# GIN stage of a four-layer graph network: ranks of edges by two passes over the bins, normalisations that read PSUM, y's bias rows in banks of their own

## The chip, the cores and the metric

One core of a Trainium2 chip runs the whole program in one launch. The metric is the device time in microseconds (us) of an execution, median of several. The engines are TensorE (PE; its weight loads are PEld), VectorE (DVE), ScalarE (ACT), GpSimd (POOL) and SyncE (SP), each with a queue of its own that is worked off in order; a wait holds everything behind it in the same queue.

## What is computed

Four graph networks in a row, each with a residual sum and a layer norm behind it, on 3125 nodes of 128 features and 53125 edges (sorted by target). The change touches the first one, GIN, of four layers:

```python
def _bn(x, g, b):
    m = jnp.mean(x, axis=0)
    v = jnp.var(x, axis=0)
    return g * (x - m) * jax.lax.rsqrt(v + BN_EPS) + b
src, dst = (edge_index[0], edge_index[1])
for l in range(L):                                      # L = 4, hidden width 32
    S = jax.ops.segment_sum(X[src], dst, num_segments=N_NODES)
    Z = (1.0 + eps[l]) * X + S
    h = jax.nn.relu(_bn(Z @ W1[l].T + b1[l], g1[l], bt1[l]))
    h = jax.nn.relu(_bn(h @ W2[l].T + b2[l], g2[l], bt2[l]))
    X = h @ W3[l].T + b3[l]
...
x = _layernorm(x + _L0_gnn_ref(x, ...), axis=-1)
x = _layernorm(x + _L1_gnn_ref(x, edge_attr_64, ...), axis=-1)
x = _layernorm(x + _L2_gnn_ref(x, ...), axis=-1)
x = _layernorm(x + _L3_gnn_ref(x, edge_attr_20, ...), axis=-1)
```

The fourth network needs the edges in another order, by source. The kernel sorts them itself, and does so inside the GIN stage.

## The kernel before

The program is a row of stages with a barrier of all engines between them: `prepare`, `adjacency`, `gin`, `layernorm`, and then the other networks. A stage ends when the last of its queues is through.

`prepare` and `adjacency` make the dense matrix of edge counts `adj` (3125 by 3125, f16, 25 tiles of 125 source nodes) in SBUF. `prepare` also leaves, in `extra`, the tables of the ranks: `bins` (125 partitions by 425 columns, f32: the bin, source // 125, of each edge), and two triangular bf16 matrices `before` and `upto`.

`gin` does two things at once.

**The layers.** The 3125 nodes stand as four groups of 32 features over up to 875 columns, so that a layer's hidden values h fill 128 partitions. A layer l makes y (per slot of 125 nodes, 32 wide; L884 for l = 0, L892 after), in PSUM banks 0 and 1; splits it in parts (`parts`, L748 to L750, or `parts16`, L745); multiplies the 25 slots with `adj`, in 7 pieces of up to 450 columns in banks 0 to 6 (L908, L917; L924); copies the sums to SBUF (pieces 0, 2, 4 by ScalarE, L817; pieces 1, 3, 5, 6 by VectorE, L774); and merges them to z in banks 7 and 0 (L943, L951). Then come two normalisations: ScalarE adds the bias and moves z from PSUM to `zb` in SBUF (L823), VectorE takes statistics of `zb` (L713 to L716), TensorE spreads mean and variance over the groups (L875, L877), VectorE makes scale and shift, ScalarE applies them with a relu (L829). Between the two stands the product by W2 (L959). Bias rows for the next y are put in banks 0 and 1 (L968) when the second normalisation has left PSUM. After the last layer L974 makes X, and L787, L833 add its bias.

**The ranks.** For each of 25 bins u in turn: VectorE marks the edges of the bin (`hots`, L664), TensorE counts with `before` and `upto` (two products of 426 columns, L848 and L849), ScalarE copies the counts (L796), VectorE scans along the 426 columns, carrying on from the bin before (L672), and chooses the marked ones (L679); GpSimd adds them to `places_f` (L641). Four bins run ahead of the layers, the other 21 are interleaved with the first layer's product, one per slot, TensorE putting the counts between the slots. Between the fourth and the fifth, VectorE makes the joined weights (L732 to L738). The 7 copies of sums of the first layer wait for the last bin (`s_placed` at L767 and L810). Then VectorE turns the places into row numbers (L777 to L781).

SP's queue in this stage: the loads, x first; a wait for all 7 copies (L614, L615); the row of degrees to HBM (L616); the places to HBM (L618); and then it fills, in 14 turns of 8 chunks, rows of edge data and places. GpSimd's queue, behind the 25 adds: 14 x 8 = 112 indirect DMAs (L647) that write 125 edge rows each to `edge_rows`. The remaining 313 are done in a later stage (L1637). The wait for places that opens this is:

```python
eng.wait_ge(s_sa, len(ACT_P))
eng.wait_ge(s_sv, len(DVE_P))
eng.dma_start(G["deg_row"][:, :], S[3 * GH:3 * GH + 1, :]).then_inc(s_deg, 16)
eng.wait_ge(s_places, 1)
eng.dma_start(places[:, :], place_i).then_inc(s_saved, 16)
eng.wait_ge(s_saved, 16)
```

## Time and profile before

| | us |
|---|---|
| median of 3 runs (2288.94 to 2290.55) | 2289.44 |
| the profiled execution | 2289.18 |
| its span in the trace | 2287.5 |
| mean granted TensorE clock, share of full | 0.782 |
| `prepare` and `adjacency` | 0 to 242.99 |
| `gin` | 242.99 to 528.03 |
| busy over the span: PE, DVE, ACT, POOL | 81%, 60%, 51%, 59% |

Times in rows are from the start of the span. A row of the timeline has start, duration, engine (SPq is a DMA issue by SyncE), line, operation, what it writes and reads, how often it stands there, and in brackets how long its engine had been idle and what ended that. The TensorE clock has two levels, 1.2 and 2.4 GHz; PEclk is the mean of what was granted, 1.00 being the higher.

### The profile page before, as it was taken

The page shows a single profiled execution, that of the slowest core. Times are in us where ns is not written, and L with a number is a line of the kernel's source. Part 1 is how long each engine was busy: PE and PEld are TensorE (multiplying, and loading weights), DVE is VectorE, ACT ScalarE, POOL GpSimd, SP SyncE. Part 2 cuts the span into 40 slices and gives each one's busy share as a digit, 9 for nine tenths or more (in the row PEclk, how much of TensorE's full clock was granted, in tenths as well). Part 3 has the DMA queues.
Part 4 walks back from the last instruction along what each step waited for, and adds up shares of the span by engine and source line. Part 5 has one row for each costly group of instructions (what it writes and reads, how often), then busy time and mean ns, then how long its engine had stood idle before and what let it go on. Part 6 is the DMA issues. An engine that isn't in the chain of part 4 may idle for free. (4 is left out here: it accounts for less than half of the span.)

```text
span 2287.5 us, 41999 instructions
## 1 busy us (share of the span) xinstructions
PE 1858.7 (81%) x8353; PEld 1333.2 (58%) x8353; DVE 1371.2 (60%) x4157; ACT 1169.0 (51%) x2626; POOL 1353.6 (59%) x1334
## 2 busy tenths in 40 slices
PE   3888677776799899999889989989986666767767
PEld 2666444445788888888555545545564454555544
DVE  6999592223444444444366576577557777777775
ACT  2999112222566666676353083073035666666663
POOL 1000136771677777777147877777726777777771
PEclk9999697887655555555679999999987777677787
DMA  0000101112344444444211111111142222222221
GB/s 12 0 0 0 45 1 18 18 17 65 96 120 118 119 119 120 119 121 121 62 40 18 19 16 18 20 17 17 20 147 67 64 64 65 64 65 65 64 65 41
DMA packets 193722, 128.61 MB, mean 56 GB/s; under 512 B 138397, under 2 KB 174886, under 8 KB 192753
## 3 DMA queue, kind: packets, MB, share of 16 engines
q0 software_dynamic: 40256, 60.21, 12.1%
q1 hardware_dynamic: 150631, 59.16, 10.1%
q10 hardware_dynamic: 2636, 7.10, 0.9%
q8 instruction: 62, 1.02, 0.2%
q14 instruction: 137, 1.12, 0.2%
HBM read 106.83 MB, written 13.34 MB: 53 GB/s over the span
## 5 line engine op out<-in xcount | busy, mean ns | idle before, releaser
L2210 POOL DMA_INDIRECT adj<-h_rows,adj x416 | 395.7, 951 | 154.9 <-issue 74.0
L1250 POOL DMA_INDIRECT extra<-p_rows,small x416 | 393.8, 947 | 136.6 <-issue 106.8
L1637 POOL DMA_INDIRECT edge_rows<-pay,small x313 | 381.7, 1219 | 98.7 <-issue 94.6
L1445 PE MATMUL ps<-work 128*128 x1024 | 302.5, 450 | 50.5 <-ACT work L1381 47.4
L2427 PE MATMUL ps<-adj 128*128 128x125 f32 x928 | 208.8, 363 | 157.9 <-DVE adj L2305 155.7
L2427 PEld LDWEIGHTS ps<-adj 128*128 128x128 f32 x928 | 172.1, 255 | 255.4 <-issue 161.2
L1445 PEld LDWEIGHTS ps<-work 128*128 128x128 f32 x1024 | 235.0, 318 | 75.4 <-issue 73.3
L1324 DVE TENSOR_TENSOR work<-ps,extra 128x256 f32<-128x256 f32 x256 | 108.7, 425 | 239.0 <-PE ps L1445 213.1
L1456 PEld LDWEIGHTS ps<-small,work 128*128 128x128 f32 x1024 | 243.6, 326 | 1.7 <-issue 0.7
L1456 PE MATMUL ps<-small,work 128*128 128x64 f32 x1024 | 240.8, 390 | 0.6 <-issue 0.5
L1999 PE MATMUL ps<-adj,work 125*128 (+2 forms) x1008 | 205.9, 361 | 21.2 <-DVE work L1728 21.2
L1999 PE MATMUL ps<-adj,extra 125*128 (+2 forms) x1092 | 214.9, 352 | 0.0
L487 PE MATMUL ps<-work 125*125 125x500 bf16 x628 | 162.8, 402 | 39.6 <-DVE work L418 39.1
L2417 PE MATMUL ps<-adj 112*128 112x256 f32 x464 | 190.1, 502 | 1.0 <-ACT adj L2350 1.0
L2295 DVE SCALAR_TENSOR_TENSOR adj<-adj 128x128 f32<-128x128 f32 x464 | 143.9, 350 | 67.3 <-POOLq L2215 55.6
L1378 ACT ACTIVATE work<-work 64x256 f32<-64x256 int32 x256 | 129.2, 505 | 84.9 <-DMA work<-edge_attr 81.1
L1999 PEld LDWEIGHTS ps<-adj,work 125*128 (+1 forms) x1008 | 100.4, 100 | 119.7 <-issue 29.1
L487 PEld LDWEIGHTS ps<-work 125*125 125x125 bf16 x628 | 114.7, 192 | 87.9 <-DVE work L418 63.3
L1999 PEld LDWEIGHTS ps<-adj,extra 125*128 (+1 forms) x1092 | 106.5, 98 | 101.6 <-issue 0.9
L647 POOL DMA_INDIRECT edge_rows<-pay,small x112 | 133.3, 1190 | 45.6 <-issue 45.0
L418 DVE TENSOR_SCALAR work<-work 125x500 bf16<-125x500 int16 x549 | 150.2, 360 | 0.0
L2279 DVE TENSOR_SCALAR adj<-adj 128x125 f32<-128x125 f32 x464 | 146.5, 371 | 0.6 <-issue 0.5
(417 smaller groups left out, 3066.5 us busy)
## 6 DMA issues: line engine op xcount, KB each, us to landing
work<-dst_all SPq DMA_DIRECT2D x256, 64.0 KB
work<-edge_attr SPq DMA_DIRECT2D x256, 64.0 KB
edge_rows<-pay,small POOLq DMA_INDIRECT x425, 2.7
extra<-p_rows,small POOLq DMA_INDIRECT x416
adj<-h_rows,adj POOLq DMA_INDIRECT x416
adj<-adj SPq DMA_DIRECT2D x232, 24.0 KB
pay<-edge_pay SPq DMA_DIRECT2D x106, 46.9 KB
adj<-edge_rows ACTq DMA_DIRECT2D x1, 2496.0 KB, 10.0
```

The costliest lines, as they stand in the source:

```text
L418: eng.tensor_scalar(ring[k][v], code, key_v[:, at], None, ALU.is_equal).then_inc(s_code, 1)
L487: eng.matmul(ps[0:P, parity * WG + k, 0:WCOLS], lows[k][:, v, :], ring[k][v], start=v == 0, stop=v == F - 1).then_inc(s_used, 1)
L1250: eng.indirect_dma_start(gathered[:, at:at + D], None, p_rows[:, :], bass.IndirectOffsetOnAxis(ap=src_i[:, c:c + 1], axis=0)).then_inc(s_g ...
L1445: ins = eng.matmul(PROD[v % 2][:, k * D:(k + 1) * D], kmat[b][:, k * EW:(k + 1) * EW], qw[:, bass.ds(w * D, D)], start=True, stop=True)
L1456: ins = eng.matmul(SUM[v % 2], rows[v % 2][:, k * D:(k + 1) * D], hot[v % 2][:, k * MW:(k + 1) * MW], start=k == 0, stop=k == PAIR - 1)
L1637: eng.indirect_dma_start(edge_rows[:, :], bass.IndirectOffsetOnAxis(ap=place[:, k:k + 1], axis=0), pay[:, k * ROW:(k + 1) * ROW], None).th ...
L1999: ins = eng.matmul(ps[:, j, 0:cw], part_of(p, s), cols, start=first, stop=last, skip_group_check=True)
L2210: eng.indirect_dma_start(gathered[:, at:at + D], None, h_rows[:, :], bass.IndirectOffsetOnAxis(ap=row3_i[:, c, DST_C:DST_C + 1], axis=0)). ...
L2279: ins = eng.tensor_scalar(hot[v % DEPTH][:, k * P:(k + 1) * P], iota, tile_v[:, v:v + 1], rows_t[:, bass.ds((c + k) * ROW + SRC_C, 1)], AL ...
L2295: ins = eng.scalar_tensor_tensor(msg[b][:, k * D:(k + 1) * D], soft[b][:, k * D:(k + 1) * D], rows_t[:, bass.ds((c + k) * ROW + RCUT_C, 1) ...
L2417: eng.matmul(PROD[v % DEPTH], attr_t[f % 2], w_f[:, cols], start=True, stop=True).then_inc(s_prod, 1)
L2427: ins = eng.matmul(SUM[v % 2], msg[b][:, k * D:(k + 1) * D], hot[b][:, k * P:(k + 1) * P], start=k == 0, stop=k == PAIR - 1)
```

## The change

In the ranks: a first pass marks all 25 bins and counts the edges of each bin per column with one product of 57 output rows each, all summed in one bank (TOTAL); one scan along the columns and a product with the triangular matrix give for each bin and column the first rank. These offsets are kept as two bf16 parts (multiples of 256, and the rest) in 25 + 25 rows. A second pass marks each bin again, and its ranks are `before` times the marks plus one product that picks the bin's row of offsets and puts it on all 125 partitions. VectorE chooses from PSUM. The scan per bin and ScalarE's copy go, and so does the matrix `upto`; `bins` is bf16. The second pass runs wholly beside the first layer's product, five bins ahead of the joined weights; since the ranks alternate between banks 5 and 6, pieces 5 and 6 of the product are done for all slots behind the others. The row numbers are made ahead of the copies of the sums.

In the layers: statistics and relu read PSUM, the copy to `zb` goes, and the bias goes into mean and shift. y of layers 1 to 3 lies in banks 5 and 6, its bias rows are put there around the first normalisation, and the product starts when the first half of y's parts is ready. The results of X lie in other banks. The first 16 slots of the first y come ahead of the size bounds. x is loaded in `adjacency`, whose work memory is moved for that.

```diff
+            eng.dma_start(T[0], a["x"]).then_inc(s_x_in, 16)
+            eng.wait_ge(s_x_in, 16)
...
+    TOTAL, BASE = ps[0:TWO, 5, 0:NC], ps[0:TWO, 6, 0:1]
+    RANK = [ps[0:P, 5 + h % 2, 0:NC] for h in range(NT)]
+    EARLY = 5
...
+        return 5 + b if l else b
...
+            def hots(n):
+                if n >= 4:
+                    if n - 4 < NT:
+                        eng.wait_ge(s_count, n - 3)
+                    else:
+                        eng.wait_ge(s_rank, n - 4 - NT + 1)
+                eng.tensor_scalar(hot[n % 4], bins, float(n % NT), None, ALU.is_equal).then_inc(s_hot, 1)
 
             def place_bin(h):
-                eng.wait_ge(s_steps, h + 1)
-                if h:
-                    eng.wait_ge(s_chosen, h)
-                else:
-                    eng.wait_ge(s_clear, 3)
-                eng.tensor_tensor_scan(total[h % 2], steps[h % 2], steps[h % 2], total[1 - h % 2][:, NC:NC + 1],
-                                       ALU.add, ALU.max).then_inc(s_scan, 1)
                 if h + 2 < NT:
-                    hots(h + 2)
-                eng.wait_ge(s_scan, h + 1)
-                if h >= 2:
-                    eng.wait_ge(s_placed, h - 1)
-                eng.scalar_tensor_tensor(chosen[h % 2], bins, float(h), total[h % 2][:, 0:NC], ALU.is_equal,
+                    hots(NT + h + 2)
+                if h >= 3:
+                    eng.wait_ge(s_placed, h - 2)
+                eng.wait_ge(s_rank, h + 1)
+                eng.scalar_tensor_tensor(chosen[h % 3], bins, float(h), RANK[h], ALU.is_equal,
                                          ALU.mult).then_inc(s_chosen, 1)
...
+            for n in range(NT):
+                hots(n)
+            eng.wait_ge(s_blank, 3)
+            for side in (0, 32):
+                eng.tensor_copy(chooser[side:side + NT, 0:NT], ident[side:side + NT, side:side + NT])
+                eng.tensor_copy(before_f[:, side:side + NT], before[0:NT, 0:NT])
+            eng.wait_ge(s_count, NT)
+            step(eng.tensor_copy(off, TOTAL))
+            step(eng.tensor_tensor_scan(upto, off, off, 0.0, ALU.add, ALU.max))
+            eng.nop(nofuse=True).then_inc(s_scan, 1)
...
+            hots(NT)
+            hots(NT + 1)
+            eng.wait_ge(s_base, 1)
+            step(eng.tensor_copy(base, BASE))
+            step(eng.scalar_tensor_tensor(off, upto, base, TOTAL, ALU.add, ALU.subtract))
+            step(eng.tensor_scalar(upto, off, 1.0 / 256, MAGIC, ALU.mult, ALU.add))
+            step(eng.tensor_scalar(upto, upto, -MAGIC, 256.0, ALU.add, ALU.mult))
+            eng.tensor_copy(offsets[0:32, 0:NC], upto[0:32, :]).then_inc(s_off, 1)
+            eng.scalar_tensor_tensor(offsets[32:TWO, 0:NC], upto[32:TWO, :], -1.0, off[32:TWO, :], ALU.mult,
+                                     ALU.add).then_inc(s_off, 1)
...
-                        eng.wait_ge(s_zb[n], l * 2 + r + 1)
-                    ins = eng.bn_stats(stats[0:tall, 6 * r:6 * r + 6], zb[0:tall, c0:c1])
+                        eng.wait_ge(s_z[n], l * 2 + r + 1)
+                    ins = eng.bn_stats(stats[0:tall, 6 * r:6 * r + 6], Z[r])
                 step(ins)
                 step(eng.bn_aggr(mv, stats[:, 0:12].rearrange("p (j f) -> p j f", f=6)))
                 eng.bn_aggr(mv[0:GH, :], stats[0:GH, :].rearrange("p (j f) -> p j f", f=6)).then_inc(s_var[n], 1)
                 eng.wait_ge(s_mean[n], l + 1)
-                eng.tensor_copy(mean, MEAN)
                 step(eng.tensor_tensor(delta, mv[:, 0:1], MEAN, ALU.subtract))
                 eng.scalar_tensor_tensor(within, delta, delta, mv[:, 1:2], ALU.mult, ALU.add).then_inc(s_dev[n], 1)
+                step(eng.tensor_tensor(mean, vector(3 * n, l), MEAN, ALU.add))
+                step(eng.tensor_tensor(centre, vector(3 * n, l), mean, ALU.subtract))
                 eng.wait_ge(s_sd[n], l + 1)
                 step(eng.reciprocal(scale, sd))
                 step(eng.tensor_tensor(scale, scale, vector(3 * n + 1, l), ALU.mult))
-                step(eng.tensor_tensor(tmp, mean, scale, ALU.mult))
-                eng.tensor_tensor(shift, vector(3 * n + 2, l), tmp, ALU.subtract).then_inc(s_aff[n], 1)
+                eng.scalar_tensor_tensor(shift, centre, scale, vector(3 * n + 2, l), ALU.mult, ALU.add).then_inc(s_aff[n], 1)
...
+                    for u in range(EARLY):
+                        place_bin(u)
...
-                    for u in range(EARLY_BINS, NT):
+                    for u in range(EARLY, NT):
                         place_bin(u)
                     eng.wait_ge(s_placed, NT)
+                    whole, part = places_f, place_i.bitcast(F32)
+                    step(eng.tensor_scalar(part, whole, 1.0 / EW, 0.5 / EW - 0.5, ALU.mult, ALU.add))
+                    step(eng.tensor_scalar(part, part, MAGIC, -MAGIC, ALU.add, ALU.add))
+                    step(eng.scalar_tensor_tensor(whole, part, -float(EW), whole, ALU.mult, ALU.add))
+                    step(eng.scalar_tensor_tensor(whole, whole, float(PAIR * PAIRS), part, ALU.mult, ALU.add))
+                    eng.tensor_copy(place_i, whole).then_inc(s_places, 1)
...
-                    for side, (b, c0, c1) in enumerate(SIDES):
-                        eng.wait_ge(s_z[n], l * 2 + side + 1)
-                        eng.activation(zb[:, c0:c1], ps[:, b, 0:c1 - c0], ACT.Identity,
-                                       bias=vector(3 * n, l)).then_inc(s_zb[n], 1)
                     eng.wait_ge(s_both[n], l + 1)
                     eng.activation(sd, VAR, ACT.Sqrt, bias=epsc).then_inc(s_sd[n], 1)
                     eng.wait_ge(s_aff[n], l + 1)
-                    for tall, c0, c1 in RELUS:
-                        eng.activation(h[0:tall, c0:c1], zb[0:tall, c0:c1], ACT.Relu, bias=shift[0:tall, :],
+                    for z, (tall, c0, c1) in zip(Z, RELUS):
+                        eng.activation(h[0:tall, c0:c1], z, ACT.Relu, bias=shift[0:tall, :],
                                        scale=scale[0:tall, :]).then_inc(s_h[n], 1)
...
+            eng.wait_ge(s_mark, 3)
+            for u in range(NT):
+                eng.wait_ge(s_hot, u + 1)
+                eng.matmul(TOTAL, mark[:, NT - 1 - u:NT - 1 - u + TWO], hot[u % 4], start=u == 0,
+                           stop=u == NT - 1).then_inc(s_count, 1)
+            def rank(h):
+                eng.wait_ge(s_hot, NT + h + 1)
+                if h >= 2:
+                    eng.wait_ge(s_chosen, h - 1)
+                eng.matmul(RANK[h], before, hot[(NT + h) % 4], start=True, stop=False)
+                eng.matmul(RANK[h], chooser[:, h:h + 1].to_broadcast([P, P]), offsets[:, 0:NC], start=False,
+                           stop=True).then_inc(s_rank, 1)
...
+            def bias_y(l, b, slots):
+                if l + 1 < GL:
+                    if l == 0:
+                        eng.wait_ge(s_wl, 1)
+                    row = bias_row[:, l * GH:(l + 1) * GH].unsqueeze(1).to_broadcast([1, slots, GH])
+                    eng.matmul(ps[0:P, y_bank(l + 1, b), 0:slots * GH].rearrange("p (s c) -> p s c", c=GH),
+                               one_row[:, 0:P], row, start=True, stop=False, skip_group_check=True)
...
+                        if b == 0:
+                            eng.wait_ge(s_scan, 1)
+                            eng.matmul(BASE, before_f, upto[0:NT, NC - 1:NC], start=True, stop=True).then_inc(s_base, 1)
+                            bounds()
...
-                eng.wait_ge(s_parts, l * 2 + 2)
+                eng.wait_ge(s_parts, l * 2 + (1 if l else 2))
...
+                def tile(slot, pieces):
+                    for j, c0, cw in pieces:
+                        ins = eng.matmul(ps[0:YW - 1, j, 0:cw], parts[:, slot, 0:YW - 1], adj[:, tile_of(slot), c0:c0 + cw],
+                                         start=slot == 0, stop=slot == NT - 1, skip_group_check=True)
+                        if slot == NT - 1:
+                            ins.then_inc(s_sum, 1)
...
-                    eng.wait_ge(s_steps, EARLY_BINS)
-                    for i in range(FULL):
-                        four(i, i == 0)
-                    for j, c0, cw in PIECES:
-                        eng.matmul(ps[0:YW - 1, j, 0:cw], parts[:, 4 * FULL, 0:YW - 1], adj[:, FULL, c0:c0 + cw],
-                                   start=False, stop=True, skip_group_check=True).then_inc(s_sum, 1)
+                    eng.wait_ge(s_off, 2)
+                    rank(0)
+                    for slot in range(NT):
+                        if slot + 1 < NT:
+                            rank(slot + 1)
+                        tile(slot, PIECES[0:5])
+                    eng.wait_ge(s_chosen, NT)
+                    for slot in range(NT):
+                        tile(slot, PIECES[5:])
                 else:
                     for n in range(0, NT, 2):
                         for j, c0, cw in PIECES:
+                            if n == 0 and j == y_bank(l, 1):
+                                eng.wait_ge(s_parts, l * 2 + 2)
...
-                spread(l, 0)
+                bias_y(l, 1, NT - 16)
+                mean_of(l, 0)
+                variance_of(l, 0)
+                bias_y(l, 0, 16)
...
-                spread(l, 1)
-                if l + 1 < GL:
-                    eng.wait_ge(s_zb[1], l * 2 + 2)
-                    if l == 0:
-                        eng.wait_ge(s_wl, 1)
-                    for b, s0, s1 in halves:
-                        row = bias_row[:, l * GH:(l + 1) * GH].unsqueeze(1).to_broadcast([1, s1 - s0, GH])
-                        eng.matmul(ps[0:P, b, 0:(s1 - s0) * GH].rearrange("p (s c) -> p s c", c=GH), one_row[:, 0:P], row,
-                                   start=True, stop=False, skip_group_check=True)
+                mean_of(l, 1)
+                variance_of(l, 1)
```

## Rows read from the trace of the kernel before

**Rows 1.** The timeline, where the layers and the scatters of the stage end.

```profile
514.52 0.54 DVE L787 TENSOR_SCALAR work<-ps,small 128x312 f32<-128x312 f32 x1 [0.72 <-PE ps L974]
...
523.61 1.19 POOL L647 DMA_INDIRECT edge_rows<-pay,small  x1 [0.30 <-issue]
```

**Rows 2.** The timeline of SP's DMA issues and the first scatter.

```profile
348.19 0.24 SPq L616 DMA_DIRECT2D deg_row<-work  x1
...
350.52 0.29 SPq L618 DMA_DIRECT2D places<-extra  x1
...
357.69 1.52 POOL L647 DMA_INDIRECT edge_rows<-pay,small  x1 [11.82 <-issue]
```

**Rows 3.** The timeline at the end of the first layer's product.

```profile
339.72 1.49 PE L917 MATMUL ps<-adj,work 125*97 125x450 f16 x7
...
345.90 2.20 DVE L774 COPY work<-ps 97x450 f32<-97x450 f32 x4 [1.05 <-POOL extra L641]
```

**Rows 4.** The timeline of a bin's cycle: TensorE not starved, then VectorE and GpSimd.

```profile
289.85 0.34 PE L848 MATMUL ps<-work,extra 125*125 125x426 bf16 x1
...
291.54 0.34 PE L848 MATMUL ps<-work,extra 125*125 125x426 bf16 x1
...
331.73 0.94 POOL L641 TENSOR_TENSOR extra<-extra,work 125x425 f32<-125x425 f32 x1 [1.76 <-DVE work L679]
331.75 1.81 DVE L672 TENSOR_TENSOR_SCAN work<-work 125x426 f32<-125x426 f32 x1
...
333.49 0.35 DVE L664 TENSOR_SCALAR work<-extra 125x425 bf16<-125x425 f32 x1
333.76 0.58 DVE L679 SCALAR_TENSOR_TENSOR work<-extra,work 125x425 f32<-125x425 f32 x1
...
334.45 1.81 DVE L672 TENSOR_TENSOR_SCAN work<-work 125x426 f32<-125x426 f32 x1
```

**Rows 5.** The timeline at the front: a fill, a scan ahead of an add.

```profile
242.99 1.48 POOL L631 MEMSET work<- 128x1664 f32 x1 [196.90 <-POOLq L112]
...
248.38 1.10 DVE L672 TENSOR_TENSOR_SCAN work<-work 125x426 f32<-125x426 f32 x1
248.44 1.78 POOL L641 TENSOR_TENSOR extra<-extra,work 125x425 f32<-125x425 f32 x1 [2.65 <-DVE work L679]
```

**Rows 6.** The timeline from the joined products to the joined weights' end.

```profile
258.58 0.64 PE L860 MATMUL ps<-work 128*128 128x32 f32 x2 [7.08 <-DVE work L692]
...
263.33 0.63 PE L867 MATMUL ps<-work,small 32*128 32x32 f32 x2 [1.02 <-DVE small L706]
...
278.19 0.46 DVE L750 TENSOR_TENSOR work<-work 125x288 bf16<-125x288 f32 x1
...
288.12 0.37 PE L848 MATMUL ps<-work,extra 125*125 125x426 bf16 x1 [1.84 <-DVEq L764]
```

**Rows 7.** Windows: stretch, length, busy time by engine, granted clock, DMA share, GB/s.

```profile
278.00:282.00 4.00, 3.21 (x9) 1.90 (x10) 3.73 (x17) 0.00 (x0) 0.00 (x0) 0.50 0.00 0
282.00:286.00 4.00, 4.00 (x20) 2.43 (x18) 3.77 (x26) 0.00 (x0) 0.00 (x0) 0.90 0.00 0
...
344.00:348.00 4.00, 1.50 (x2) 0.84 (x3) 2.92 (x6) 1.42 (x3) 0.94 (x1) 0.53 0.00 0
...
385.00:396.00 11.00, 11.00 (x117) 7.03 (x114) 0.00 (x0) 0.00 (x1) 8.87 (x8) 1.00 0.18 17
```

**Rows 8.** Groups by line and form: line, operation, count, busy us, mean ns.

```profile
L823 ACT ACTIVATE work<-ps,small 128x438 f32<-128x438 f32 x8 | 5.0, 625 | 21.8 <-PE ps L951 17.7 <-PE ps L959 4.1
...
L748 DVE TENSOR_TENSOR work<-ps,work 125x512 f32<-125x512 f32 x1 | 0.7, 692 | 10.3 <-ACT work L804 10.3
L750 DVE TENSOR_TENSOR work<-work 125x512 bf16<-125x512 f32 x1 | 0.7, 692 | 0.0
```

**Rows 9.** The DMA view's row of x, and GpSimd's first work in `adjacency`.

```profile
work<-x SPq DMA_DIRECT2D x1, 1562.5 KB, 6.9
...
43.59 0.54 POOL L390 IOTA work<- 125x500 int16 x1 [25.61 <-issue]
```

More of the change, by code:

```diff
@@ L51 @@
 GIN_TURNS = 14
-EARLY_BINS, FIRST_TILE = 4, 3
+TWO = 32 + NT
 LOG2 = float(np.log(2.0))
@@ L139, in build @@
         apart = Words(extra)
-        ranks = dict(bins=apart(P, NC), places_f=apart(P, NC), place_i=apart(P, NC, I32), before=apart(P, P, BF16), upto=apart(P, P, BF16))
+        ranks = dict(sources=apart(P, NC, I32), bins=apart(P, NC, BF16), places_f=apart(P, NC), place_i=apart(P, NC, I32),
+                     before=apart(P, P, BF16), one_row=apart(1, D), mark=apart(P, NT + TWO, BF16),
+                     chooser=apart(P, NT + 1, BF16), before_f=apart(NT, TWO), offsets=Words(extra)(P, NC + 1, BF16))
         phase(prepare, keep, ranks)
@@ L164, in prepare @@
     key_v, low_v, key_c, low_c, over_n = (keep[k] for k in ("key_v", "low_v", "key_c", "low_c", "over_n"))
-    hi, before, rest = (ranks[k] for k in ("bins", "before", "upto"))
+    raw_s, bins, before = (ranks[k] for k in ("sources", "bins", "before"))
     over_d = G["over_d"]
@@ L532, in gin @@
     bias_row = s_(1, (GL - 1) * GH)
-    stats, mv, sd, scale, shift, tmp = s_(D, 6 * 3), s_(D, 2), s_(D, 1), s_(D, 1), s_(D, 1), s_(D, 1)
-    epsc, delta, mean, within = s_(D, 1), s_(D, 1), s_(D, 1), s_(D, 1)
+    stats, mv, sd, scale, shift = s_(D, 6 * 3), s_(D, 2), s_(D, 1), s_(D, 1), s_(D, 1)
+    epsc, delta, mean, within, centre = (s_(D, 1) for _ in range(5))
     YW = 3 * GH + 2
```

151 lines of the change are left out of this document (50 added, 101 removed).

## The prediction

> **What bounds the kernel now.** I read first the end of the stage that the change touches. GIN runs from 242.99 us, and its last compute instruction ends at 515.06; GpSimd's last scatter of edge rows is issued at 523.61 and runs to 524.80 [rows 1]. So the stage is ended by the 112 scatters and not by the layers: the layers have 524.80 - 515.06 = 9.7 us to spare. The scatters are issued back to back, (523.61 - 357.69) / 111 = 1.495 us apart, whatever the other engines do. What counts is when the first one starts.
>
> Then I followed the scatters back. The first starts at 357.69; it needs its places, which SP first writes to HBM at 350.52 and then loads back [rows 2]. From that write to the first scatter are 7.2 us that the diff does not touch. SP's queue is in order: L616 (the row of degrees) first waits for all seven copies of the summed pieces (`s_sa`, `s_sv`), and L618 stands behind it. The copies start at 345.90, though TensorE began the last seven pieces at 339.72 [rows 3]: both copying engines first wait for `s_placed`, the 25th bin. So today the bins' ranks are the long chain.
>
> Last the cycle of one bin [rows 4]. From one scan (331.75) to the next (334.45) it is 2.70 us, and 21 bins are done so; between them stand the mask (L664) and the choice (L679). GpSimd's add (0.94 us) starts 0.02 us before the scan, and the scan then takes 1.81 us; where a scan began 0.06 us ahead of an add it took 1.10, and the add came out long, 1.78 [rows 5]: VectorE and GpSimd take turns. TensorE alone could go faster: where it doesn't starve, two rank products and seven pieces recur after 291.54 - 289.85 = 1.69 us [rows 4]. The rank products are 0.18 us each, so a piece is (1.69 - 0.36) / 7 = 0.19.
>
> **The ranks, part by part.** The scan in each bin goes, with ScalarE's copy that feeds it. What remains in a bin is a mask (0.27 us from its start to the next instruction's, 333.49 to 333.76), the choice (0.59), the add (0.94) and two rank products. New is a first pass: 25 more masks and 25 products into one bank, one copy, one scan, and the making of the offsets.
>
> Front. 25 masks at 0.27 are 6.8 us from 243.3; GpSimd's fills, about 4 us in all with the 1.48 of the largest [rows 5], take turns with them. That ends near 254. 25 count products at the half clock, 0.36 each, from 244.5 end at 253.5, so either way 254. Copy (0.6) and scan (1.1) give 255.7; the merge and fold constants are 2.2 us as before: 257.8 against 258.58 for TensorE's first joined product, 0.8 us earlier. Then the first 16 slots of y come ahead of the size bounds, so that TensorE no longer idles for `s_limits` (1.1 us ahead of 263.33); the start-of-bin product adds 0.4. The last y part, ready at 278.65 now [rows 6], is ready at 278.65 - 0.8 - 1.1 + 0.4 = 277.1. The offsets (some 2.6 us of VectorE) lie beside bounds and second half of y. I hold this step to plus or minus 2 us.
>
> Loop. TensorE now issues, per slot, two rank products and five pieces: 0.36 + 5 x 0.19 = 1.31 us. VectorE has 0.27 + 0.59, and behind that GpSimd's 0.94 with one mask in its way is 1.2: both fit in 1.31 if the choice, which now reads the rank from PSUM and one tensor from SBUF, can run while GpSimd adds. No row shows that pair. Its bounds are 1.31 (no turns) and 0.27 + 0.59 + 0.94 = 1.8 (all in turns, as scan and add do). I take 1.31: what the scan shares with the add is two reads of SBUF, and the choice has one. The Trainium skill, SBUF — State Buffer, "Who interferes with whom", says that a VectorE instruction with at most one SBUF input outside the two-port modes doesn't contend with GpSimd; the blocked scan agrees with its other half, and by it 1.31 stands.
>
> The order costs something: after five bins VectorE does the joined weights, 278.65 to 288.12 = 9.5 us [rows 6], and TensorE can go only to rank 6 and slot 5. It runs dry there for some 7 us, and idle time drops the clock: after TensorE had had next to nothing from 341.2 (339.72 + 1.49) to 346, the mean granted clock was 0.53, and the start at 278.8 ran at the lower level (1.2 GHz) until about 282.8, the window 282 to 286 showing 0.90 [rows 7]. A restart so costs about 2.2 us, and there are two, at 277.1 and behind the weights. In sum, from 277.1: five bins, 5 x 0.36 + 3 x 0.95 = 4.65, with restart 2.2 and the last choice 0.8, 7.7 us; weights 9.5; bin 5's mask and choice 0.9; 18 ranks and 19 five-piece slots 6.5 + 18.0 = 24.5; second restart 2.2; pieces 5 and 6 of all 25 slots, which had to leave their banks to the ranks and wait for the 25th choice, 50 x 0.19 = 9.4. That is 54.2 us, and TensorE ends the first layer's product at 331.3. Places are finished beside the last 9.4 us: last choice near 319.5, add 1, arithmetic 2.5, 323. So the two copies of pieces 5 and 6 (1.2 us) end last, at 332.5; degrees leave at 332.6, the places write behind it at 332.9. Against 350.52 that is 17.6 us earlier, and with it the first scatter and the stage's end.
>
> **The normalisations and y's bias rows.** 16 copies to SBUF of 0.62 us go [rows 8]; of each pair the second is on the layer's chain. With the mean's copy and one scalar step less, a normalisation is about 1.0 us shorter, 8 in all; bias rows made ahead and the product that starts with half of y give about 2 us in each of three layers. The product by w2 may overwrite a bank only behind the relu that reads it, a wait that is there already. Together 14 us, and they buy nothing: chain end 515.06 - 16 - 14 = 485 against scatters to 524.80 - 17.6 = 507.2. The cover is 22 us thick; without it, it would be the bound.
>
> Does reading PSUM cost? A subtraction of 512 columns took 692 ns from PSUM and 692 from SBUF [rows 8], so nothing. The Trainium skill, VectorE: DVE Perf Modes, the section on the TRN2 errata, has a fixed 120 cycles for a PSUM source against 58: 65 ns, which over 25 choices would be 1.6 us, beside TensorE. The rows disagree, and the sum is the same by both.
>
> **x moved to the adjacency.** 1562.5 KB, 6.9 us to land [rows 9], no longer in the way of GIN's weights, which aren't late even now. In its new place it is waited for by SP alone, 200 us ahead of need. But it starts when GpSimd, silent from the stage's barrier to 43.59, is on its way to the constants that VectorE waits for. If the transfer holds that up, the whole kernel moves by 0 to 6.9 us; I take 0, since the silence shows no transfer that it waits for.
>
> **Sum.** Against the profiled execution, 2289.18: 2289.18 - 17.6 = 2271.6. Median is 0.26 above it: 2271.8.
>
> **Rivals.**
> - The choice takes turns with GpSimd all the same: bins at 1.8 instead of 1.31. From the weights on, 20 x 1.75 puts the last rank 8.4 us later, the first five bins lose 1: 2281. For it: both engines add tensors of 425 columns. Against it: only one SBUF input. 20%.
> - The x load holds up GpSimd in the adjacency: up to +6.9, 2278.7. 8%.
> - Better than the sum: the counts keep the clock up, no restart (4.4), front 2 us shorter: 2265. For it: TensorE has the count products at 244 where it had eight. 10%.
> - Slower: the clock does not come up in the loop. All 25 x 0.36 + 175 x 0.19 = 42.3 us at half speed are 84.5, with a stall of 4 us behind the weights: product's end 365.7, places 367.3, 16.8 later than now: 2306. For it: from 258 to 282 TensorE was nearly always busy, at 0.50. Against: dense pieces ran at 1.00 from 385 to 396 [rows 7]. It decides from a mean of about 0.66 in the loop, where 33.9 us grow by 17.6. 6%.
> - The ranks' gain doesn't reach the end (layers bound instead): excluded by 22 us unless a normalisation grows by 2.7 us; with other ways to land within 0.2%, 5%.
>
> **Numbers.** The forecast, 2271.8 (own range 2267 to 2276), has 51%. The range to 2 in 10 outside takes in the turns case and the fast one: 2264 to 2283. About 0.2% (4.6 us) is what a measurement can tell from no change; faster by more 0.88, within 0.05, slower 0.07.
>
> **What would show it.** The first scatter at about 340 us and 112 of them still 1.49 apart; the stage ends some 22 us behind the last layer's output; places write right behind the degree row, which waits for pieces 5 and 6. Per-bin spacing of the choice 1.3, not 1.8; a TensorE gap of 7 us during the weights, with a low clock behind it. Bn statistics start right at the product's end. I am wrong if the choice lasts over 1 us, if the stage of the adjacency grows, or if the scatter starts after 352.

## The result, and the profile after

The changed kernel takes 2275.97 us (median of four runs, 2271.17 to 2279.41) beside 2289.19 (2287.02 to 2290.55): ratio 0.9941, 95% interval 0.9923 to 0.9959. On a later chip ten runs gave 2275.00 and a ratio of 0.9946 (0.9933 to 0.9959). The forecast was 2271.8, in a range of 2264 to 2283; the median lies inside the range and 4.2 us above the forecast. The profiled execution took 2278.92, with a span of 2277.2.

The end of the stage, from the timeline of the changed kernel (start, length in us, engine, line, operation; the idle time before it and what ended it in brackets), against [rows 1]:

```profile
487.69 0.54 DVE L808 TENSOR_SCALAR work<-ps,small 128x312 f32<-128x312 f32 x1 [0.72 <-PE ps L987]
...
507.14 1.18 POOL L660 DMA_INDIRECT edge_rows<-pay,small  x1 [0.30 <-issue]
511.55 0.37 SPq L1028 DMA_DIRECT2D small<-mlp_w1a  x1
```

The third line is the first DMA issue of the next stage. The last scatter is issued 16.47 us earlier than the 523.61 of [rows 1], and the next stage begins 16.5 us earlier than the 528.03 of before. The layers end at 488.2, 20.1 us under the scatters' 508.3; the forecast had 485 and a cover of 22.

What starts the scatters, against [rows 2]:

```profile
333.84 0.25 SPq L622 DMA_DIRECT2D deg_row<-work  x1
334.13 0.29 SPq L624 DMA_DIRECT2D places<-extra  x1
...
341.24 1.52 POOL L660 DMA_INDIRECT edge_rows<-pay,small  x1 [17.84 <-issue]
```

The places leave at 334.13 instead of 350.52: 16.4 us, where 17.6 were forecast. They stand right behind the degree row, which waits for pieces 5 and 6 of the product:

```profile
321.37 11.39 PE L922 MATMUL ps<-adj,work 125*97 125x450 f16 x60
...
323.43 0.38 DVE L791 TENSOR_SCALAR extra<-extra 125x425 f32<-125x425 f32 x1 [1.20 <-POOL extra L654]
...
325.54 0.38 DVE L795 CAST extra<-extra 125x425 int32<-125x425 f32 x1
325.84 1.15 DVE L802 COPY work<-ps 97x450 f32<-97x450 f32 x2
332.62 1.13 DVE L802 COPY work<-ps 97x450 f32<-97x450 f32 x2 [5.63 <-PE ps L922]
```

The places' own arithmetic is done at 325.9. For the next 8.2 us they wait in SyncE's queue for two copies that they don't need (the experiment below takes this away).

The cycle of one bin, where [rows 4] had 2.70 us between two scans:

```profile
305.80 0.60 DVE L683 SCALAR_TENSOR_TENSOR work<-extra,ps 125x425 f32<-125x425 bf16 x1 [0.54 <-PE ps L856]
306.31 0.27 DVE L675 TENSOR_SCALAR work<-extra 125x425 bf16<-125x425 bf16 x1
306.47 1.08 POOL L654 TENSOR_TENSOR extra<-extra,work 125x425 f32<-125x425 f32 x1 [0.39 <-DVE work L683]
307.12 0.60 DVE L683 SCALAR_TENSOR_TENSOR work<-extra,ps 125x425 f32<-125x425 bf16 x1 [0.54 <-PE ps L856]
```

From choice to choice it is 1.32 us, and VectorE waits 0.54 in each for TensorE. The choice at 307.12 takes 0.60 us, as all 25 do (0.59 to 0.60), while GpSimd's add, begun at 306.47, goes on.

Windows of the changed kernel (stretch, length, busy time and count by engine, granted clock, DMA share, GB/s), against [rows 7]:

```profile
277.00:281.00 4.00, 3.98 (x11) 2.42 (x12) 1.97 (x4) 0.00 (x0) 2.02 (x2) 0.50 0.00 0
281.00:285.00 4.00, 4.00 (x17) 2.52 (x16) 1.59 (x5) 0.00 (x0) 1.60 (x2) 0.73 0.01 2
...
290.00:297.00 7.00, 0.03 (x1) 0.07 (x2) 6.51 (x41) 0.00 (x0) 0.10 (x1) 0.74 0.00 1
297.00:301.00 4.00, 4.00 (x13) 2.41 (x14) 2.64 (x6) 0.00 (x0) 2.86 (x3) 0.60 0.00 0
301.00:333.00 32.00, 32.00 (x171) 21.54 (x170) 16.07 (x39) 1.42 (x3) 16.83 (x17) 1.00 0.00 1
```

Here are both starts at the low level (1.2 GHz), the gap of TensorE while VectorE makes the joined weights, and 32 us of unbroken work at the full 2.4 GHz. TensorE is idle for 8.5 us in that gap (288.48 to 296.97), where 7 were forecast.

### The profile page after: what moved, and what is told of

Its sections match the earlier page's. It is cut to its first block and busy times, and to the rows that moved or that the text cites. A ratio compares the mean times of both kernels' runs of the same rounds, so it can differ in the third digit from the quotient of the medians.

```text
span 2277.2 us, 41982 instructions
## 1 busy us (share of the span) xinstructions
PE 1858.6 (82%) x8380; PEld 1338.7 (59%) x8380; DVE 1341.6 (59%) x4164; ACT 1145.5 (50%) x2585; POOL 1355.0 (60%) x1338
## 5 line engine op out<-in xcount | busy, mean ns | idle before, releaser
L2430 PE MATMUL ps<-adj 112*128 112x256 f32 x464 | 184.4, 488 | 1.0 <-ACT adj L2363 1.0
```

Of the source, the lines that this page charges most:

```text
L2430: eng.matmul(PROD[v % DEPTH], attr_t[f % 2], w_f[:, cols], start=True, stop=True).then_inc(s_prod, 1)
```

## The experiments

Each edit stood beside the kernel before on one chip. The first run of the changed kernel once more, of each half alone and of places first fell on a chip on which the kernel before takes 2807.19 us (the slow chip); in all later ones it takes 2287.8 to 2292.4 (usual chips). Times and ratios are compared within one chip; traces of different usual chips are also set side by side, and in three of them the changed kernel's next stage begins at 511.55, 511.80 and 510.63.

Each of these four kernels also has a later profile, from a usual chip (spans of 2263 to 2290 us); the lines and times called those of the slow chip are from its own profiles. In the later ones the layers end at 487.8 (changed kernel), 498.1 (ranks half), 501.6 (normalisation half) and 487.3 (places first), and the next stage begins at 510.6, 511.1, 527.3 and 502.6: everywhere behind the scatters, as in the runs on usual chips below.

**The changed kernel once more.** No edit.

> The changed kernel once more, nothing edited. In the profiled run of the first measurement the stage ended 16.5 us earlier than before, but the program only 10.3 us earlier, and its last 50 small products of the interaction stage took 9.33 us at a granted clock of 0.50 where those of the kernel before took 6.55 us at 1.00. Theory A: what is given back behind the stage is partly a matter of how the clock's steps fall in the last 20 us and varies from run to run; this kernel's times then spread over 5 us or more again, and a profile whose time is near 2271 shows these 50 products at 1.00 and 6.6 us. Theory B: the loss is fixed by the program; every run of it then lies within 2 us of 2276 and a profile shows 9.3 us there again. Median under both: 2272 to 2278.

Measured: 2783.52 beside 2807.19, ratio 0.9922 (0.9895 to 0.9949). This chip was slower by over a fifth with the same program, so the 2272 to 2278 of the expectation didn't apply, but the run showed another thing. The end of the stage on it:

```profile
506.42 1.19 POOL L660 DMA_INDIRECT edge_rows<-pay,small  x1 [0.30 <-issue]
...
515.49 0.54 DVE L808 TENSOR_SCALAR work<-ps,small 128x312 f32<-128x312 f32 x1 [0.72 <-PE ps L987]
517.04 0.37 SPq L1028 DMA_DIRECT2D small<-mlp_w1a  x1
```

The scatters are where they were, and the layers end last, at 516.0. Up to the places (333.5) nothing differs by more than 1 us; from layer 1 on TensorE is late. This kernel's timeline there:

```profile
379.47 1.00 PE L954 MATMUL ps<-work 128*128 128x438 f32 x2
382.58 0.55 ACT L828 ACTIVATE work<-ps 128x450 f32<-128x450 f32 x1 [22.47 <-remote]
383.18 6.21 PE L968 MATMUL ps<-work 128*128 128x438 f32 x8 [2.70 <-ACT work L828]
```

and the same three steps in the first profile of the changed kernel:

```profile
377.55 1.42 ACT L828 ACTIVATE work<-ps 128x450 f32<-128x450 f32 x3 [16.53 <-PE ps L944]
...
378.58 1.00 PE L954 MATMUL ps<-work 128*128 128x438 f32 x2
...
379.42 3.10 PE L968 MATMUL ps<-work 128*128 128x438 f32 x8
```

The copy of the first summed piece starts 5.0 us later, 3 us after the recorded end of the product (the ends of products are modelled). TensorE then waits for the copy, and its next eight products take twice as long: 6.21 us instead of 3.10. Why the product is late on this chip no record shows.

**The ranks half alone.** The normalisations read biased copies in SBUF again; y's bias rows go behind both, in their old banks.

```diff
+                    for side, (b, c0, c1) in enumerate(SIDES):
+                        eng.activation(zb[:, c0:c1], ps[:, b, 0:c1 - c0], ACT.Identity, ...)
-                    ins = eng.bn_stats(stats[0:tall, 6 * r:6 * r + 6], Z[r])
+                    ins = eng.bn_stats(stats[0:tall, 6 * r:6 * r + 6], zb[0:tall, c0:c1])
...
-                bias_y(l, 1, NT - 16)
                 mean_of(l, 0)
                 variance_of(l, 0)
-                bias_y(l, 0, 16)
```

> The changed kernel with the second half of the change undone: the normalisations read their biased copies in SBUF again, and y's bias rows are written behind both normalisations, in the banks that they had. Theory (all of the gain comes through the places): layers end some 14 us later than the changed kernel's 488.2, near 502, still 6 us under the last scatter's 508.3; the stage ends at the same 511.5, and the time is that of the changed kernel within 0.2% (2272 to 2278). Rival (the normalisations carry a part of the gain, or the layers come so near that they collide with the scatters): the stage ends 1 to 6 us later and the time is 2279 to 2285.

> Once more the changed kernel with its normalisation half undone. On the chip of the first four runs the layers, not the scatters, ended last (516.0 against 507.6 in the changed kernel), and this kernel's stage ended at 529.2 instead of 517.0. There a TensorE product of the layers ran slower than its records say: after the last product of layer 1 (379.5) the copy of its first piece started only at 382.6, in the first profiled run of the changed kernel at 377.6 and before the last product ended. Theory: which path ends last is a matter of how fast the chip's TensorE is; if this call's chip takes 2289 for the kernel before, the layers end near 502, the scatters near 508 to 511 and the stage ends within 1 us of 511.5 plus whatever this kernel starts later by; the time is 2272 to 2279, ratio 0.993 to 0.996. If it takes some 2807 again, as before: stage end 529, ratio 0.994. Rival: the normalisations carry 12 us on every chip: stage end 523 or later, ratio 0.999.

Measured on the slow chip: 2796.65, ratio 0.9939 (0.9907 to 0.9971), with the next stage at 529.2 instead of 517.0, 12 us later; neither theory nor rival had that. On a usual one: 2274.65, ratio 0.9933 (0.9911 to 0.9954). Its stage end:

```profile
497.10 0.54 DVE L808 TENSOR_SCALAR work<-ps,small 128x312 f32<-128x312 f32 x1 [0.72 <-PE ps L991]
...
506.85 1.18 POOL L660 DMA_INDIRECT edge_rows<-pay,small  x1 [0.30 <-issue]
511.28 0.37 SPq L1032 DMA_DIRECT2D small<-mlp_w1a  x1
```

The layers end 9.4 us later than with both halves, and the stage ends 0.3 earlier (its places left 0.5 earlier). So where the scatters end last the normalisation half is worth nothing to the time, and the ranks half is the whole gain; where the layers end last the normalisation half is worth 12 us of the stage.

**The normalisation half alone.** The same edit, put into the kernel before.

> The kernel before with the second half of the change alone: normalisations read PSUM, y's bias rows go ahead into other banks; ranks as before. Theory: layers end some 14 us earlier than before, near 500, but the scatters still end near 525 and the next stage starts at 528; the time is that of before within 0.2% (2285 to 2293). Rival: the layers set a part of the end; the next stage starts 3 to 14 us earlier and the time is 2275 to 2284.

> The kernel before with the normalisation half alone, once more, for the chip on which the scatters end last. With the ranks half alone (2274.65, ratio 0.9933) the stage ended at 511.3 there, and the layers 9.4 us later than with both halves. Theory where the kernel before takes 2289: layers end 10 us earlier than before's 515.1, near 505, scatters as before, the next stage starts at 528 as before; ratio 0.999 to 1.001. Rival: the stage ends by more than 2 us earlier, ratio under 0.998. Where the kernel before takes 2807: 0.997 again, stage end 531 with the layers last.

Measured on the slow chip: 2800.11, ratio 0.9976 (0.9957 to 0.9995); the layers end at 530.4 and the next stage begins at 531.4. On a usual one: 2290.64 beside 2287.76, ratio 1.0011 (0.9998 to 1.0023), from

```profile
503.12 0.54 DVE L793 TENSOR_SCALAR work<-ps,small 128x312 f32<-128x312 f32 x1 [0.72 <-PE ps L984]
...
522.95 1.19 POOL L653 DMA_INDIRECT edge_rows<-pay,small  x1 [0.30 <-issue]
527.37 0.37 SPq L1025 DMA_DIRECT2D small<-mlp_w1a  x1
```

The layers end 11.4 us earlier than the 515.06 of before, and nobody waits for them. The next stage comes 0.7 us early; GpSimd's first work in the adjacency stage came 0.8 us early too (42.8), so this is put down to the front of that stage.

**Places first.** SyncE's queue in another order.

```diff
-            eng.wait_ge(s_sa, len(ACT_P))
-            eng.wait_ge(s_sv, len(DVE_P))
-            eng.dma_start(G["deg_row"][:, :], S[3 * GH:3 * GH + 1, :]).then_inc(s_deg, 16)
             eng.wait_ge(s_places, 1)
             eng.dma_start(places[:, :], place_i).then_inc(s_saved, 16)
             eng.wait_ge(s_saved, 16)
-            eng.wait_ge(s_deg, 16)
             for b in SETS:
                 fill(0, b)
+            eng.wait_ge(s_sa, len(ACT_P))
+            eng.wait_ge(s_sv, len(DVE_P))
+            eng.dma_start(G["deg_row"][:, :], S[3 * GH:3 * GH + 1, :]).then_inc(s_deg, 16)
...
+            eng.wait_ge(s_deg, 16)
```

> The changed kernel with SyncE's queue in another order: it waits for the places, writes them and issues the first fills, and only then waits for the pieces of the product and writes the row of degrees. In the changed kernel the places' arithmetic was done at 325.9 and the write issued at 334.1, behind the degrees' 333.8. Theory (the queue's order holds the places for 8 us): the write is issued at 326, first scatter at 333, the stage ends at 503.5, and the time is 8 us under the changed kernel's, 2264 to 2270, if the layers (488) stay under the scatters' end (500). Rival (the edge rows' or the degrees' transfers, or the layers under contention, end last instead): the first scatter moves but the stage's end moves by less than 4 us, 2271 to 2277.

> Places first in SyncE's queue, once more, since on the chip of the first call the layers and not the scatters ended last. Where the kernel before takes 2289, theory (scatters end last, layers at 488): first scatter at 333.4 instead of 341.2, last issued at 499.4, stage end 503.8 instead of 511.5, time 7 to 8 us under the changed kernel's: 2265 to 2269, ratio 0.989 to 0.991. Rival (the layers, beside the earlier scatters, end last): stage end above 506.

Measured on the slow chip: 2774.38, ratio 0.9890 (0.9865 to 0.9914). The scatters ended at 500.7, but the next stage began at 514.3, behind the layers' 513.3, and so only 2.7 us earlier: the rival held there. On a usual chip: 2268.18, ratio 0.9921 (0.9896 to 0.9947), beside the changed kernel's 2275.00 and 0.9946:

```profile
325.42 0.30 SPq L621 DMA_DIRECT2D places<-extra  x1
...
332.68 1.52 POOL L660 DMA_INDIRECT edge_rows<-pay,small  x1 [9.81 <-issue]
333.31 0.22 SPq L627 DMA_DIRECT2D deg_row<-work  x1
...
498.83 1.19 POOL L660 DMA_INDIRECT edge_rows<-pay,small  x1 [0.30 <-issue]
503.25 0.37 SPq L1028 DMA_DIRECT2D small<-mlp_w1a  x1
```

The stage ends at 503.3 instead of the 511.8 of the changed kernel in the same session, 8.5 us earlier, so the order of the queue was the wait. The medians differ by 6.8.

**Joined weights last.** Places first, and VectorE makes the nine columns of joined weights behind all 25 choices and the places' arithmetic; TensorE waits for them (`s_wl`) ahead of the merging products.

```diff
-                    for u in range(EARLY):
+                    for u in range(NT):
                         place_bin(u)
+                    eng.wait_ge(s_placed, NT)
+                    ...
+                    eng.tensor_copy(place_i, whole).then_inc(s_places, 1)
                     eng.wait_ge(s_bound, 1)
...
-                    for u in range(EARLY, NT):
-                        place_bin(u)
...
+                    if l == 0 and side == 0:
+                        eng.wait_ge(s_wl, 1)
```

> The changed kernel with places first in SyncE's queue, and with the nine columns of joined weights moved behind all 25 choices and the places' arithmetic on VectorE, so that the product of the first layer has no gap at bin 5 and no second start at the low clock. Theory for a chip on which the kernel before takes 2289 (scatters end last): the choices end near 310 instead of 321.6, the places are written near 315.5 instead of 334.1, the last scatter is issued near 489 and the stage ends near 493; the layers, whose product ends near 321 instead of 332.8, end near 478 to 482, still under the scatters; time 14 to 18 us under the changed kernel's 2276: 2257 to 2263, ratio 0.986 to 0.989. For a chip like the one of the last four runs (before 2807; layers end last, at 516): the scatters end 16 us under the layers; the stage ends with the layers, 5 to 10 us earlier than 517 there: 507 to 512. Rival: the weights, now between the choices and the copies of the product's pieces, hold the copies by their 9.5 us; the layers end as before, and the gain is only that of places first.

Measured: 2255.31, ratio 0.9850 (0.9828 to 0.9873). The window that held the gap, and the stage's end:

```profile
285.00:297.00 12.00, 12.00 (x65) 8.15 (x64) 7.17 (x19) 0.00 (x0) 9.00 (x10) 1.00 0.00 0
```

```profile
315.56 0.30 SPq L621 DMA_DIRECT2D places<-extra  x1
...
480.21 0.54 DVE L806 TENSOR_SCALAR work<-ps,small 128x312 f32<-128x312 f32 x1 [0.72 <-PE ps L987]
...
488.69 1.19 POOL L660 DMA_INDIRECT edge_rows<-pay,small  x1 [0.30 <-issue]
493.11 0.37 SPq L1028 DMA_DIRECT2D small<-mlp_w1a  x1
```

The gap and the second slow start are gone, places leave at 315.56 (315.5 expected) and the stage ends at 493.1 (493). The layers start their merging products at 324.9. The weights hold them, as the rival said, but by 2.7 us and not 9.5, so they still start 7.7 us earlier than the changed kernel's 332.60 and end at 480.8 instead of 488.2. The time is 2 us under the expected 2257 to 2263.

**The choice from SBUF.** ScalarE copies each rank to SBUF, and the choice reads both operands there.

```diff
-                eng.scalar_tensor_tensor(chosen[h % 3], bins, float(h), RANK[h], ALU.is_equal,
+                eng.scalar_tensor_tensor(chosen[h % 3], bins, float(h), ranked[h % 2], ALU.is_equal,
...
+                        eng.activation(ranked[u % 2], RANK[u], ACT.Copy).then_inc(s_read, 1)
```

> The changed kernel with one more step in each bin of ranks: ScalarE copies the ranks from PSUM to SBUF, and the choice on VectorE reads both of its operands in SBUF instead of one of them in PSUM. In the changed kernel the choice (0.60 us) and GpSimd's addition (0.94 us) of the bin before overlapped, with a cycle of 1.32 us set by TensorE. Theory (they overlap because the choice has one operand in PSUM; with both in SBUF it takes turns with GpSimd, as the old scan did): a cycle of at least 0.60 + 0.35 (mask) + 0.94 = 1.8 to 1.9 us; 18 bins behind the weights take 9 to 10 us longer, and the places are written near 343 instead of 334. Rival (no turns for these forms at all, neither in PSUM nor in SBUF): the cycle stays at 1.32 to 1.4 and the places stay within 2 us of 334.

Measured: 2275.37, ratio 0.9936 (0.9915 to 0.9958). The groups of this kernel from 309 to 321 us, and below them those of the changed kernel from 301 to 320 (count, busy us, mean ns):

```profile
L655 POOL TENSOR_TENSOR extra<-extra,work 125x425 f32<-125x425 f32 x8 | 10.8, 1344 | 1.5 <-DVE work L684 0.5
L676 DVE TENSOR_SCALAR work<-extra 125x425 bf16<-125x425 bf16 x9 | 8.6, 957 | 0.0
L684 DVE SCALAR_TENSOR_TENSOR work<-extra,work 125x425 f32<-125x425 bf16 x9 | 6.2, 690 | 0.0
```

```profile
L654 POOL TENSOR_TENSOR extra<-extra,work 125x425 f32<-125x425 f32 x15 | 14.8, 988 | 5.7 <-DVE work L683 5.7
L683 DVE SCALAR_TENSOR_TENSOR work<-extra,ps 125x425 f32<-125x425 bf16 x15 | 9.0, 598 | 8.8 <-PE ps L856 8.8
L675 DVE TENSOR_SCALAR work<-extra 125x425 bf16<-125x425 bf16 x14 | 3.8, 269 | 0.0
```

With two operands in SBUF, mask and add grow by 0.69 and 0.36 us, and the cycle (309.40 to 321.18 for eight bins) is 1.47 us. Turns are real for this pair, and the PSUM operand avoids them. But they cost 0.15 us a bin and not the 0.5 of the expectation: choice and add alone come to 0.59 + 0.94 = 1.53, and the mask, which the expectation added to them, isn't a term of the cycle. The places' arithmetic ends 3.1 us later (328.97 instead of 325.92), yet the places leave only 1.3 us later (335.4), since pieces 5 and 6 still end last; with places first in the queue the turns would be expected to show more. The program's time shows nothing. The Trainium skill, SBUF — State Buffer, "Who interferes with whom", says that a VectorE instruction with two SBUF inputs contends with a GpSimd instruction that reads SBUF and one with a single input doesn't; the two kernels agree with both halves.

**x loaded in the old place.**

```diff
-            eng.dma_start(T[0], a["x"]).then_inc(s_x_in, 16)
-            eng.wait_ge(s_x_in, 16)
...
+            eng.dma_start(T[0], a["x"]).then_inc(s_x_in, 16)
             for dst, src in ((w1, a["gin_w1"]), ...
...
+                    eng.wait_ge(s_x_in, 16)
```

> The changed kernel with the load of x put back at the head of this stage's DMA queue, from the front of the adjacency stage; TensorE waits for it before y. The changed kernel's adjacency stage started its first GpSimd work at 44.9 instead of 43.6 and the stage with the ranks at 244.5 instead of 243.0. Theory (x, loaded first, holds the adjacency's first loads): the first GpSimd work is back at 43.1 to 43.8, the stage with the ranks starts at 243.0 and everything up to the places is 1.4 us earlier, as x lands some 7 us after its issue and before TensorE's 258. Rival (the difference is how the first loads happen to land; the four runs so far show 44.6, 46.0, 43.1 and 45.3 with the first, second and fourth of them having x first): this run shows anything from 43 to 46 and no fixed shift.

Measured: 2271.32 (two runs, 2270.16 and 2272.47), ratio 0.9917 (0.9889 to 0.9945). GpSimd's first work in the adjacency stage, in this kernel, then in the changed one:

```profile
42.78 0.54 POOL L388 IOTA work<- 125x500 int16 x1 [24.79 <-issue]
```

```profile
36.05 0.37 SPq L384 DMA_DIRECT2D work<-x  x1
44.90 0.54 POOL L390 IOTA work<- 125x500 int16 x1 [26.88 <-issue]
```

Of fourteen profiles, nine with x loaded first have it at 44.6 to 46.0, five without at 42.5 to 43.6 [rows 9 has 43.59]; in the four later ones it is 44.2 to 44.5 with x first and 42.85 without. The sets don't overlap, so the rival falls. The means of the fourteen are 45.0 and 43.0: x costs the whole kernel 2.0 us there, and here the next stage begins at 509.6 instead of 511.6. What GpSimd waits for while x is in flight no view shows. The medians give more than the 2.0 (3.7 us under the changed kernel's 2275.00 on another chip), but they rest on two runs.

**The changed kernel a third time, and all three edits together.**

> The changed kernel a third time, nothing edited, so that the two edits below have it beside them on one chip. Expected where the kernel before takes 2289: 2271 to 2280, stage end within 1 us of 511.5, and if its profiled run is near 2271, the 50 small products near the end take 6 us and not 9.3. Where it takes 2807 as in the first call: 2776 to 2797, stage end 517 with the layers last.

> Places first, joined weights behind the choices, and x's load back at the head of this stage's queue, together. Where the kernel before takes 2289: with x out of the adjacency's first loads its first GpSimd work started at 42.8 instead of 44.6 to 46.0 and the stage end moved by 2.0 (509.6 against 511.6). Theory: the three add up, as all lie ahead of the first scatter: stage end 493.1 minus 2.0 = 491, time 2253 (2251 to 2256), ratio 0.983 to 0.985. Rival (x, issued 4 DMA issues and some 12 us ahead of its first use, becomes late once the loads of weights share its queue, or the gain is only noise of the first loads): 2255 or more. Where it takes 2807: 0.984 to 0.988.

Measured: 2275.00 for the changed kernel (2270.65 to 2278.76, ratio 0.9946), and 2253.44 (2252.80 to 2257.02) for all three edits, ratio 0.9858 (0.9832 to 0.9883), 21.6 us under it in one session. The next stage begins at 490.3, as the sum of the three parts says (491). The time met its expectation; the ratio lies just above the expected 0.983 to 0.985. Against the version without the x edit (0.9850 on another chip) its time can't be told apart; only the traces show the 2 to 3 us. Places first with weights last is a kernel 35 to 37 us faster than the one before.

The 50 small products near the end, one line of the view by source line for each (shortest, median and longest in ns, first and last start): in the kernel before, the changed kernel's first profile and its third.

```profile
L2468 PE MATMUL ps<-small,work x50: 168/248/350, 2268.5 to 2274.7; 128*125 128x1 f32 x50
```

```profile
L2481 PE MATMUL ps<-small,work x50: 167/348/349, 2254.8 to 2263.8; 128*125 128x1 f32 x50
```

```profile
L2481 PE MATMUL ps<-small,work x50: 167/248/350, 2249.9 to 2256.4; 128*125 128x1 f32 x50
```

From first to last start: 6.2, 9.0 and 6.5 us. In the later profile of the changed kernel, with a span of 2270.5, it is 5.9. The same code takes either length, by how many of its products fall at the low clock (the median is 348 ns in the long one, 248 in the short ones); so theory A stands and B falls. It isn't the whole spread: places first had 8.8 here in the fastest of its four runs.

## Why the prediction was right

- **The number.** The forecast lies 4.2 us under the median. The stage gave 16.5 us instead of 17.6, which is 1.1 of it; the other 3 lie behind the stage. Two larger misses inside the stage cancelled, at its front.
- **What bounds the stage: right.** 112 scatters, (507.14 - 341.24) / 111 = 1.495 us apart, end last, and the half that leaves them alone changed nothing (ratio 1.0011). On the slow chip it was not so: there the layers end last. The cover of 22 us, called thick, was eaten there by 28 us of slower layers.
- **Front: right in its number by luck.** The first rank product starts at 277.02, forecast 277.1, though the stage began 1.4 us late, at 244.4. That the stage of the adjacency grows was one of the prediction's own signs of being wrong, and it did grow. Within GIN the front was 1.5 us shorter than worked out: the 25 masks beside GpSimd's fills took 9.5 us (244.76 to 254.29) where some 10.7 were reckoned. Of the faster rival, one half came: with the count products the granted clock was 0.95 from 252 to 256, but it was back at 0.50 from 260 on, so both low starts of the loop stayed.
- **Loop: right in its rule, with small misses that add up.** From 277.02 the five bins took until 285.49, 8.5 us (7.7 forecast: the clock came up only near 283); the weights until 296.04, 10.6 (9.5); bin 5 0.9 (0.9); the rest until 332.76, 35.8 (36.1). The product ended 1.5 us after the forecast 331.3. The turns rival did not come, and its price was too high: with turns forced, a bin took 1.47 us and not 1.8, as the mask is no term of that sum, and most of the rest hid beside pieces 5 and 6.
- **PSUM reading costs next to nothing: right.** The choice took 597 ns in the mean with the rank from PSUM (and `bins` in bf16), and 585 in the kernel before with both operands in SBUF (and `bins` in f32); bn_stats over 438 columns took 621 ns against 616 from SBUF. The 65 ns of the Trainium skill's errata table (VectorE: DVE Perf Modes) appear in neither.
- **x at nothing: the term that was mis-sized.** I took 0 from bounds of 0 to 6.9; it is 2.0 us in the mean of the profiles. [rows 9] already spoke for a price: GpSimd's silence ended at 43.59, and x's transfer (issued at 36.05, with 6.9 us to land in its old place) lies in that time. "The silence shows no transfer that it waits for" was no reason, as the profile doesn't show what it waits for. With x in its old place the changed kernel takes 2271.32, where 2271.8 was forecast; that this is so near is in part luck, as the 3 us behind the stage were no term of the forecast.
- **Normalisations 14 us: the mechanism right, the size not.** From the product's end (332.6) to the layers' 488.2 are 155.6 us; with copies, from 332.0 to 497.6, 165.6: 10.0 us. In layer 0 ScalarE's table load (1.28 us) now lies on the chain; it used to lie behind the copies:

```profile
345.92 1.28 ACT L833 ACT_TABLE_LOAD   x1 [21.07 <-PE ps L893]
347.21 0.26 ACT L833 ACTIVATE small<-ps,small 128x1 f32<-128x1 f32 x1
```

  In the ranks half alone it starts at 343.42, beside the spreading of mean and variance, and ends 1.3 us before the standard deviation is computed. The second normalisation of layer 0 became 0.8 us shorter and not 1.0: TensorE's idle time ahead of its mean went from 1.92 to 1.27, and from there to the relu it takes 2.71 instead of 2.85. From the relu to the next product it is 4.35 instead of 6.22, so 1.9 for y, with 2 forecast. If all eight and all three are like these, 8 x 0.8 + 3 x 1.9 - 1.3 = 10.8. Of the 4 us between 14 and 10.0 the table load is then 1.3, the normalisations (0.8 instead of 1.0, eight times) 1.6, y 0.3, and 0.8 stays open; none of it cost time here.
- **The sum through the rest of the program: open by 3 us.** The stage gave 16.5 us and the medians 13.2 and 13.3. From the next stage's first issue to the end, ten profiles of nine kernels on chips of 2289 (the one before among them) take 1757 to 1766 us, with no trend in where the stage ended. In the first profile of the changed kernel it was 1765.6, before 1759.5. The 50 products hold 3 us of that. Whether 3 us in the medians are chance too isn't settled: all three edits gave 37.8 us at the stage's end and 34.9 in the median, weights last 34.9 and 37.1.

## What to carry to other kernels

When a stage ends with a chain of fixed length, only its start counts: follow the start back through every queue in order, and look for waits that stand ahead of it in the queue and have no business with it. Here such an order was worth 8.5 us of the stage and filling TensorE's gap another 10, as much together as the whole change. A load put into an idle-looking stretch has a price until a profile of both places says otherwise. Shortening a path that isn't the last to end is insurance and not gain: it was worth nothing on the usual chips and 12 us of the stage on the slow one.

## What the runs showed of the hardware

- Chips differ in more than a factor: the same program took 2275 to 2276 us on two and 2784 on a third. Up to 333 us the two traces agree within 1 us, with TensorE at its full clock in long stretches of both (1.00 from 100 to 240 us); behind that a product of the slow chip was late by 3 us against its own record, and another path ended the stage. The cause is open.
- GpSimd's add (0.94 us where nothing of VectorE holds it) beside a VectorE choice with two SBUF operands takes 1.34 us in the mean, and a bf16 mask beside it 0.96 instead of 0.27. The choice took 0.59 where its record begins 0.1 us ahead of the add (310.84 and on) and up to 1.52 (at 307.78) where the add began first. With a PSUM operand in the choice it kept 0.59 to 0.60 in all 25 bins, and the add 0.94 to 1.09.
- The mask has one input, and yet it took turns as well where an add was already running: 0.74, 0.55 and 0.67 us at 279.22, 297.42 and 298.53 of the changed kernel, against 0.27 where it began ahead of the add. Beside GpSimd's fills the first four masks of the stage took 3.49 us, the other 21 together 5.95.
- GpSimd's first instruction of the adjacency stage came 2.0 us later in the mean when x's 1562.5 KB had been issued at 36.05 (44.2 to 46.0 us against 42.5 to 43.6), though none of its operands is among them. The cause is open.
